# Differential attention with an expert layer on one core: where the attention rows are split into high and low parts, who combines the two maps, and which bank the query products use

## The reference

```python
A1 = jnp.einsum('bhqd,bhkd->bhqk', Q1, K1) * scaling
A2 = jnp.einsum('bhqd,bhkd->bhqk', Q2, K2) * scaling
attn = jax.nn.softmax(A1, axis=-1) - lam * jax.nn.softmax(A2, axis=-1)
O = jnp.einsum('bhqk,bhkd->bhqd', attn, V)
rms = jnp.sqrt(jnp.mean(O * O, axis=-1, keepdims=True) + EPS)
O = O / rms * rms_scale
...
return jnp.einsum('bne,de->bnd', O, Wo)
...
x = _layernorm(x + _L0_attn_ref(x, ...), axis=-1)
x = _layernorm(x + _L0_ffn_ref(x, ...), axis=-1)
```

## Time and profile before

| | |
|---|---|
| median of 3 runs | 1050.59 us (1050.27 to 1050.68) |
| profiled execution | 1053.84 us, span 1052.1 us |
| PE busy | 890.3 us (85%) |
| PEld busy | 720.4 us (68%) |
| POOL busy | 793.4 us (75%) |
| DVE busy | 766.6 us (73%) |
| ACT busy | 581.0 us (55%) |
| granted TensorE clock, mean | 0.925 |

### The profile page before, as it was taken

The page is one execution under the profiler, slowest core; times in us unless marked ns, Lnnn a source line. Parts: engine busy times, 40 slices in busy tenths (PEclk is TensorE's granted clock), DMA queues, the critical chain, the costliest instruction groups (busy, mean ns, idle before and its releaser), DMA issues.

```text
span 1052.1 us, 15341 instructions
## 1 busy us (share of the span) xinstructions
PE 890.3 (85%) x4365; PEld 720.4 (68%) x4366; DVE 766.6 (73%) x1185; ACT 581.0 (55%) x1090; POOL 793.4 (75%) x875
## 2 busy tenths in 40 slices
PE   6789999999999999999999999999999741258710
PEld 5567778887887788778877887878788531146510
DVE  6678778877887878788778878888788548536504
ACT  3546667666766576656766666766676331124300
POOL 2567888887988798888888888888799753375881
PEclk9899999999999999999999999999999955569955
DMA  2000000000000000000000000100000142011334
GB/s 70 1 11 11 1 1 19 3 1 0 20 0 0 10 10 0 0 10 10 0 0 10 10 0 0 50 0 0 1 1 1 53 130 65 19 51 26 33 35 122
DMA packets 36000, 20.67 MB, mean 20 GB/s; under 512 B 4560, under 2 KB 34416, under 8 KB 35968
## 3 DMA queue, kind: packets, MB, share of 16 engines
q1 hardware_dynamic: 30336, 15.95, 5.4%
q0 software_dynamic: 5632, 4.33, 3.0%
HBM read 13.85 MB, written 6.42 MB: 19 GB/s over the span
## 4 chain that ended last, share of the span: by engine, by line
PE 53%; issue 18%; DVE 16%; POOL 5%; ACT 3%; DMA 2%; another core or an unknown queue 2%; DVEq 0%; POOLq 0%; ACTq 0%; SPq 0%
PE t_ps L1074 7%; DVE negmax L760 6%; PE ring_a L1007 5%; PE ring_b L1007 5%; PE ring_a L1009 5%; PE ring_a L1008 5%; PE ring_b L1009 4%; PE ring_b L1008 4%; PE u_ps L1007 4%; PE u_ps L1008 4%; PE u_ps L1009 4%; POOL acc_dram L500 3%; ACT prob L572 2%; PE o_ps L1007 2%
## 5 line engine op out<-in xcount | busy, mean ns | idle before, releaser
L459 POOL TENSOR_TENSOR at_lo<-at,at_hi 128x1024 fp32r<-128x1024 f32 x127 | 308.6, 2430 | 0.8
L572 ACT ACTIVATE prob<-ring_a,negmax 128x1024 f32<-128x1024 f32 x128 | 142.8, 1116 | 252.7 <-DVE negmax L760 252.7
L431 POOL TENSOR_TENSOR s1sq<-psum 128x1 f32<-128x1 f32 x127 | 104.2, 820 | 125.2 <-ACT at L580 123.1
L828 DVE SCALAR_TENSOR_TENSOR attn<-prob,coef 128x1024 f32<-128x1024 f32 x128 | 180.1, 1407 | 5.1
L760 DVE TENSOR_REDUCE negmax<-ring_b 128x1 f32<-128x1024 f32 x128 | 155.6, 1216 | 4.7 <-PE ring_b L1009 1.7
L760 DVE TENSOR_REDUCE negmax<-ring_a 128x1 f32<-128x1024 f32 x128 | 155.7, 1216 | 1.3 <-PE ring_a L1009 0.2
L572 ACT ACTIVATE prob<-ring_b,negmax 128x1024 f32<-128x1024 f32 x128 | 142.8, 1116 | 20.3 <-DVE negmax L760 17.8
L434 POOL TENSOR_SCALAR at_hi<-at 128x1024 fp32r<-128x1024 f32 x127 | 141.4, 1114 | 0.0
L1074 PE MATMUL t_ps<-ident,attn 128*128 128x128 f32 x1024 | 134.4, 274 | 3.5 <-DVE attn L828 3.1
L1074 PEld LDWEIGHTS t_ps<-ident,attn 128*128 128x128 f32 x1024 | 118.9, 141 | 26.2 <-DVE attn L828 12.1
L580 ACT ACTIVATE at<-t_ps 128x1024 f32<-128x1024 f32 x128 | 130.2, 1017 | 2.7 <-PE t_ps L1074 2.7
(11 more groups left out here) (241 smaller groups left out, 1709.8 us busy)
## 6 DMA issues: line engine op xcount, KB each, us to landing
at<-in_L_ffn_w SPq DMA_DIRECT2D x16, 256.0 KB, 3.2
xres<-in_L_attn_X SPq DMA_DIRECT2D x2, 512.0 KB, 4.5
wq_s<-in_L_attn_Wq SPq DMA_DIRECT2D x8, 128.0 KB, 2.1
wk_s<-in_L_attn_Wk SPq DMA_DIRECT2D x8, 128.0 KB, 2.2
wv_s<-in_L_attn_Wv SPq DMA_DIRECT2D x8, 128.0 KB, 2.1
wo_s<-in_L_attn_Wo SPq DMA_DIRECT2D x8, 128.0 KB, 2.4
acc_dram<-zero SPq DMA_DIRECT2D x1, 1024.0 KB, 5.1
xg_dram<-xres SPq DMA_DIRECT2D x2, 512.0 KB, 3.4
```

The source lines that it names most:

```text
L431: pool.tensor_tensor(s1sq[:, r % TPH:r % TPH + 1], s1, s1, ALU.mult).then_inc(s1sq_ready, 1)
L459: pool.tensor_tensor(at_lo[:, g, :, c], src, at_hi[:, g, :, c].bitcast(F32), ALU.subtract).then_inc(at_split, 1)
L572: act.activation(prob[:, par, m, :], ring[m][:, :], ACT.Exp, bias=negmax[:, par, m:m + 1], accum_out=sums).then_inc(prob_ready, 1)
L828: dve.scalar_tensor_tensor(out=attn[:, par, :], in0=prob[:, par, 1, :], scalar=coef[:, par:par + 1], in1=prob[:, par, 0, :], op0=ALU.mult, ...
```

## The change

The transposes of a row come in two halves of four, both in the first bank of `t_ps`; ACT writes `at_hi` of a half straight from that bank (`at_high`) and DVE `at_lo` (`at_low`), so `at32`, the copy and POOL's two splits are gone. The second bank of `t_ps`, called `x_ps`, holds every extra product: a query chunk at the end of slots 0, 1, 3, 4 and 9, 11, 12, 15, m in 5, wt in 7, wp in 8; ACT and DVE read it at the beginning of the next slot. DVE's three operations of the combination go to POOL as five: a power (1/sum2) and two multiplications for the coefficient, a scaling of map 2 in place, and an addition. `attn` has four row buffers. The ages change: map 2's exponential one slot later (`LAG_E`), the coefficient 1, combination 2, transposes 2 and 3, product with x 7, output product 12, y 12, layer norm 0 two tail slots later. `es1` is made for four rows at once. Elsewhere `at32` is replaced by attn's buffers 2 and 3, whose loading waits for the last transposes.

```diff
 
-    LAG_T = 1
-    LAG_U = 6
-    LAG_O = 10
-    LAG_Y = 11
...
-
-    AT_QB, AT_WT, AT_WP, AT_M, AT_QA = (1, 2), 4, 6, 9, (11, 13)
-
-    AT_LN = (18, 19, 20, 21, 22)
...
+    LAG_E = 1
+    LAG_C = 1
+    LAG_S = 2
+    LAG_T1 = 2
+    LAG_T2 = 3
+    LAG_U = 7
+    LAG_O = 12
+    LAG_Y = 12
+    AB = 4
...
+    X_QB = {0: (0, 0), 1: (1, 0), 3: (0, 1), 4: (1, 1)}
+    X_M, X_WT, X_WP, AT_WW = 5, 7, 8, 11
+    X_QA = {9: (0, 0), 11: (1, 0), 12: (0, 1), 15: (1, 1)}
+
+    AT_LN = (20, 21, 22, 23, 24)
...
-        attn = sb("attn", [P, 2, N])
-        at32 = sb("at32", [P, 2, N])
+        attn = sb("attn", [P, AB, N])
...
         ring = [ps("ring_a", [P, N]), ps("ring_b", [P, N])]
         t_ps = ps("t_ps", [P, N])
+        x_ps = t_ps[:, NC:2 * NC]
...
+                r = i - LAG_S
...
+                    ts, sp = t - LAG_S, r % 2
                     s1 = psum1[:, r % TPH:r % TPH + 1]
+                    pool.wait_ge(coef_ready, ts + 1)
...
                     pool.tensor_tensor(s1sq[:, r % TPH:r % TPH + 1], s1, s1, ALU.mult).then_inc(s1sq_ready, 1)
-                    c = slice((r % GT) * P, (r % GT + 1) * P)
-                    src = at32[:, par, :].rearrange("p (k q) -> p k q", q=P)
-                    pool.tensor_scalar(at_hi[:, g, :, c], src, 1.0, 0.0, ALU.mult, ALU.add).then_inc(at_hi_done, 1)
-                r = i - LAG_O
+                    pool.tensor_scalar(prob[:, sp, 1, :], prob[:, sp, 1, :], coef[:, sp:sp + 1], None,
+                                       ALU.mult).then_inc(scaled_ready, 1)
+                    pool.wait_ge(scaled_ready, ts + 1)
+                    pool.tensor_tensor(attn[:, r % AB, :], prob[:, sp, 1, :], prob[:, sp, 0, :],
+                                       ALU.add).then_inc(attn_ready, 1)
...
+                    tc, par = t - LAG_C, r % 2
+                    need(pool, attn_ready, tc - 1)
+                    pool.wait_ge(prob_ready, 2 * tc + 2)
+                    pool.tensor_tensor(rs2[:, par:par + 1], psum2[:, par:par + 1], neg_one[:, :],
+                                       ALU.pow).then_inc(rs2_ready, 1)
+                    pool.wait_ge(rs2_ready, tc + 1)
+                    pool.tensor_tensor(coef_1[:, par:par + 1], rs2[:, par:par + 1], psum1[:, r % TPH:r % TPH + 1],
+                                       ALU.mult).then_inc(coef_1_ready, 1)
...
+                    pool.wait_ge(coef_1_ready, tc + 1)
+                    pool.tensor_tensor(coef[:, par:par + 1], coef_1[:, par:par + 1], neglam_h[:, :],
+                                       ALU.mult).then_inc(coef_ready, 1)
...
-                    pool.tensor_tensor(at_lo[:, g, :, c], src, at_hi[:, g, :, c].bitcast(F32),
-                                       ALU.subtract).then_inc(at_split, 1)
...
+            def q_round(h, which, m, c, src):
...
+                act.wait_ge(q_ready, q_count(h, which, m, c))
+                act.activation(q_hi[:, b, m, c * NC:(c + 1) * NC], src, ACT.Copy).then_inc(q_hi_done, 1)
...
+                def at_high(half, lag):
+                    r = i - lag
...
+                        act.wait_ge(t_ready, 2 * ta + half + 1)
...
+                        act.activation(at_hi[:, g, half * GT:(half + 1) * GT, c],
+                                       t_ps[:, 0:NC].rearrange("p (k q) -> p k q", q=P),
+                                       ACT.Copy).then_inc(at_hi_done, 1)
...
+                at_high(0, LAG_T1 + 1)
+                if not tail and i - 1 in X_QB:
+                    q_round(h, "b", *X_QB[i - 1], x_ps)
...
+                exponential(1, LAG_E)
...
-                    act.wait_ge(t_ready, tt + 1)
-                    need(act, at_split, tt - 1)
-                    act.activation(at32[:, r % 2, :], t_ps[:, :], ACT.Copy).then_inc(t_copied, 1)
...
+                at_high(1, LAG_T2)
+                exponential(0, 0)
...
+                def at_low(half, lag):
+                    r = i - lag
...
+                        dve.wait_ge(at_hi_done, 2 * ta + half + 1)
+                        dve.tensor_tensor(at_lo[:, g, k, c], t_ps[:, 0:NC].rearrange("p (k q) -> p k q", q=P),
+                                          at_hi[:, g, k, c].bitcast(F32), ALU.subtract).then_inc(at_split, 1)
...
+                at_low(0, LAG_T1 + 1)
+                if not tail and i - 1 in X_QB:
+                    q_part(h, "b", *X_QB[i - 1], x_ps)
...
+                at_low(1, LAG_T2)
+                if not tail:
+                    row_max(1)
...
-                    dve.reciprocal(rs2[:, par:par + 1], psum2[:, par:par + 1]).then_inc(rs2_ready, 1)
-                    dve.wait_ge(rs2_ready, t + 1)
-                    dve.tensor_scalar(coef[:, par:par + 1], rs2[:, par:par + 1], psum1[:, i:i + 1],
-                                      neglam_h[:, :], ALU.mult, ALU.mult).then_inc(coef_ready, 1)
-                    dve.wait_ge(coef_ready, t + 1)
-                    need(dve, t_ready, t - 1)
-                    dve.scalar_tensor_tensor(out=attn[:, par, :], in0=prob[:, par, 1, :],
-                                             scalar=coef[:, par:par + 1], in1=prob[:, par, 0, :],
-                                             op0=ALU.mult, op1=ALU.add).then_inc(attn_ready, 1)
...
+                def transposes(half, lag):
+                    r = i - lag
...
+                        if half == 0:
+                            pe.wait_ge(attn_ready, tt + 1)
+                        need(pe, at_split, 2 * tt + half)
+                        for k in range(GT):
+                            kk = half * GT + k
+                            last_t = pe.transpose(t_ps[:, k * P:(k + 1) * P], attn[:, r % AB, kk * P:(kk + 1) * P],
+                                                  ident[:, :])
+                        last_t.then_inc(t_ready, 1)
...
+                if not tail:
+                    scores(0, 0)
...
+                if not tail:
+                    scores(0, 1)
+                output()
+                transposes(1, LAG_T2)
+                if not tail:
+                    scores(1, 0)
+                    scores(1, 1)
+                r = i - LAG_U
...
+                    for k in range(j * PER, (j + 1) * PER):
...
+                transposes(0, LAG_T1)
+
+                if not tail and i in X_QB:
+                    m, c = X_QB[i]
+                    pe.wait_ge(q_split, q_count(h, "b", m, c) - 1)
+                    q_product("b", m, c, x_ps)
...
+                    m_product(h + 1, x_ps)
...
+                if i in X_QA and not last:
+                    m, c = X_QA[i]
...
+                    q_product("a", m, c, x_ps)
...
-                put_in = [i == AT_QB[0] and not tail, i == AT_QA[0] and not last, i == AT_WP and not tail,
-                          i == AT_M and not last]
-                if any(put_in):
-                    pe.wait_ge(prob_ready, 2 * t + 1)
```

More of the change, by code:

```diff
@@ L420, in slot @@
                 t = TPH * h + i
[L421 to L428 removed]
+                r = i - LAG_S
+                if exists(h, r, first) and r < TPH:
+                    ts, sp = t - LAG_S, r % 2
@@ new lines, in slot @@
+                at_low(0, LAG_T1 + 1)
+                if not tail and i - 1 in X_QB:
+                    q_part(h, "b", *X_QB[i - 1], x_ps)
+                if not last and i - 1 in X_QA:
+                    q_part(h + 1, "a", *X_QA[i - 1], x_ps)
+                if i == 0 and not first:
+                    q_part(h, "a", *X_QA[TPH - 1], x_ps)
+                if not last and i - 1 == X_M:
+                    m_parts(h + 1, x_ps[:, 0:2 * D])
+                if not tail and i - 1 == X_WT:
+                    dve.wait_ge(wt_ready, h + 1)
+                    need(dve, ww_installed, 2 * h)
+                    dve.tensor_copy(wwn_hi[:, 0:DV], x_ps[:, 0:DV]).then_inc(wt_hi_done, 1)
+                    for m in range(2):
+                        dve.tensor_scalar(wot_s[:, m, :], x_ps[:, DV + m * D:DV + (m + 1) * D],
+                                          rms_c[:, m:m + 1], None, ALU.mult).then_inc(wt_split, 1)
+                    dve.wait_ge(wt_hi_done, h + 1)
+                    dve.tensor_tensor(wwn_lo[:, 0:DV], x_ps[:, 0:DV], wwn_hi[:, 0:DV].bitcast(F32),
+                                      ALU.subtract).then_inc(wt_split, 1)
@@ L766, in slot @@
-                if r % GT == 0 and exists(h, r, first) and r < TPH:
-                    g = GPH * h + r // GT
-                    dve.wait_ge(u_hi_done, g + 1)
-                    dve.tensor_tensor(u_lo[:, :], u_ps[:, :], u_hi[:, :].bitcast(F32),
-                                      ALU.subtract).then_inc(u_split, 1)
-                if not tail:
-                    row_max(1)
                 if first and i == 0:
@@ L831, in slot @@
[L831 to L843 removed]
+                if i == 0 and not first:
+                    head_lambda()
@@ new lines, in output @@
+                def output():
+                    r = i - LAG_O
+                    if exists(h, r, first) and r < TPH:
```

(52 more changed lines are left out.)

328 lines of the change are left out of this document (136 added, 192 removed).

## The result

| | before | after |
|---|---|---|
| median | 1050.43 us, 4 runs (1042.34 to 1050.68) | 1192.89 us, 4 runs (1190.83 to 1195.81) |
| profiled execution, span | 1053.84, 1052.1 us | 1194.24, 1192.5 us |
| DVE, ACT, POOL busy | 766.6, 581.0, 793.4 us | 704.6, 592.1, 1022.7 us |

The change made the kernel slower: ratio of the mean times 1.138, 95% interval 1.132 to 1.144. The forecast was 1006 us.

The account below looks back on a forecast made before the run. TensorE was taken as the bound, at 95.6 us a head plus waits. Gains 15 + 25.8 + 4.2 + 0 = 45 us took 1053.8 to 1008.8 profiled, 1006 us median; forecast 999 to 1018, range 999 to 1036.

Parts of the forecast that it names:

- POOL's slot: POOL's work per slot after the change: 5.70 us, against TensorE's mean slot of 5.98, 0.28 us to spare.
- the one-input row: POOL's at_hi in the trace of before, 1.05 us, taken as the price of the new per-row scaling.
- the two-input row: POOL's at_lo in the trace of before, 2.40 us, taken as upper bound for the new scaling.
- rival 2: POOL becomes the bound: scaling at 2.40 us makes its slot 7.05 us, +102, 1153 us; chance 0.09.
- TensorE's price of a head: TensorE's work in one head, 16 slots of 5.54 us plus 7.0 us of extra products: 95.6 us.
- The gain of 25.8 us: Heads 1 to 6: the own bank removes TensorE's waits of 4.3 us a head.
- Head 0: First head, paced by POOL, then TensorE: 85.7 us against 102.3, 16.6 saved, taken as 15.
- Rival 3: Head 0 does not gain: ramp waits on hand-overs, 5.8 us a slot, 7 us lost, 1013 us; no separate chance given.
- Last head: The last head's 15 slot steps: 86.8 us instead of 91.0, 4.2 us gained.
- The handoff of the halves at nothing: Both transpose halves pass through one bank: 1.75 us under 1.9 us of cover, cost nothing, 0.15 us of room.
- Rival 1: The one bank of the two transpose halves becomes the wait: 1022 to 1038 us with 0.2 to 0.4 missing; chance 0.25.
- Tail: From the last scores to the second layer norm: 29.5 us against 30.7, counted as 0, between -2 and +3.

Follow-up runs that it names:

- the version with the second operation: The changed kernel with plus 0.0 added as second operation to POOL's scaling by the per-row coefficient: 1006.19 us, median of 5; ratio to before 0.963.
- two immediates: The changed kernel with POOL scaling map 2 by constant -0.25 and adding 0.0, per-row coefficient left out of the result: 1001.9 us.
- four forms of at_hi: The kernel before, POOL's at_hi written by slot number with an immediate or a column of ones, each with and without plus 0.0: 1122.1 us.
- the split version: The changed kernel, DVE combining columns 0 to 511, POOL the rest: 1004.13 us with a single-operation scaling, 1014.75 with two operations.

## Why the prediction was wrong

**The step that failed** is one term of POOL's slot: "Lower bound: the one-input row, 1.05 us; upper bound: the two-input row, 2.40. I take 1.05, since it reads one tensor and writes one like at_hi." It measured 2.86 us, above the upper bound too. I had chosen the row by the number of tensors, and asked only whether a per-row scalar differs from an immediate. At_hi's row was a pair of operations, times 1.0 and plus 0.0; the new instruction is a single one. The pair looked like two steps of which one is idle, and its plus 0.0 like a formality. The trace of before has no TENSOR_SCALAR with a single operation on POOL, so no row could price it. The range missed because it left out rival 2 altogether: even at its 2.40 us the time would have been 1153. Rival 2 had the mechanism right (POOL without gaps, the exponential of map 1 behind it) at a price of 2.40; its working with 2.86 gives 7.51 us a slot, measured 7.40. Its 127 slots at the full price overstate head 0, whose first slots lack var_o and fac (104.2 us): 940 us by the formula, 925.4 measured.

**The other steps**, read in the version with the second operation, whose profiled execution took 1006.19 us (span 1004.4). Row maxima of map 1:

```profile
L786 DVE TENSOR_REDUCE negmax<-ring_a x16: 1214/1225/1227, 22.5 to 100.2; 128x1 f32<-128x1024 f32 x16
L786 DVE TENSOR_REDUCE negmax<-ring_a x97: 1211/1225/1227, 106.6 to 680.4; 128x1 f32<-128x1024 f32 x97
L786 DVE TENSOR_REDUCE negmax<-ring_a x16: 1214/1225/1226, 680.4 to 767.3; 128x1 f32<-128x1024 f32 x16
```

- *TensorE's price of a head*, 95.6 us: (680.4 - 106.6) / 6 = 95.6. The gain of 25.8 us is there (25.7).
- *Head 0*: 84.1 us against 102.3, 18.2 saved where I had worked out 16.6 and taken 15. Rival 3 didn't come (and by its own figures it would have cost 7 x 5.8 - 34.7 = 5.9 us, not 7).
- *Last head*: 86.9 us; 86.8 was forecast.
- *POOL's slot*: 5.69 us, forecast 5.70. The scaling takes 1.13 rather than 1.05; the slot shown has no es, and smaller steps make up the rest. s1sq takes 0.19 us, undisturbed.
- *The handoff of the halves at nothing*: no wait of TensorE for at_lo stands in the table of waits from 107 to 680 us, which holds only waits of ACT, DVE and POOL. Rival 1 fell; with ACT busier by a scaling no such wait appears either.
- *Tail*: from the last of these starts to the second layer norm it is 805.72 - 767.3 = 38.4 us, against 844.00 - 812.8 = 31.2 before: 7.2 us lost where I counted 0 and at worst 3. Measured as in the earlier trace rows, from the last score matmul, it is 805.72 - 769.23 = 36.5 against 30.7; map 2's scores now come later in the slot, which is the other 1.4. My chain for it was too short (its terms add up to 29.4). POOL ended the last row 10.4 us after the scores, as I had said; but two halves through ACT and DVE, counted at 3.5, ended only 5.8 us later. So the last at_lo ends 16.1 us after the scores against 11.5 before, 4.7 of the 5.8 us. With the combination on DVE it was 16.3, so POOL's pace isn't the reason; the granted clock isn't either (0.91 in this stretch against 0.92 before, and with two immediates, at 1.00 throughout, from the last of the starts it took 36.8 us).
- *What no step spoke of*: behind that layer norm the profiled execution of before took 208.1 us and this one 198.7, for the same work. Most of it lies in the expert stage, whose low parts span 70.6 us in the one and 61.7 in the other:

```profile
L969 DVE TENSOR_TENSOR q_lo<-attn,q_hi x32: 691/693/768, 922.6 to 993.2; 128x512 fp32r<-128x512 f32 x32
```

```profile
L979 DVE TENSOR_TENSOR q_lo<-attn,q_hi x32: 691/693/768, 884.9 to 946.6; 128x512 fp32r<-128x512 f32 x32
```

In the kernel before with four forms of at_hi it was 61.2 us (1001.1 to 1062.3), and in all other profiled executions 60.5 to 65.9, so this is not the change but that one execution: before itself took anything from 1041 to 1053 us. The forecast took 45 us from a long one, 1053.84; against the runs of before beside it (1043.93) the version with the pair gains only 37.7. That it lands on 1006.19 is in part luck: between the two profiled spans the heads gain 48.0 us, the part ahead of them loses 2.5, and behind them the shorter expert stage, which the change didn't make, hides the tail's loss and leaves a gain of 2.2.

**The rule of the Trainium skill** (GPSIMD Engine Reference, 4.1 Engine selection) that spoke against the move holds by the outcome of the change as written. It adds that GpSimd is about at line rate with one input; the runs agree for a pair of operations and for a copy (1.05 and 1.04 us for 1024 columns) and disagree for a single operation (2.78). With the pair the move is right although POOL spends 3.5 us for DVE's 1.3, since POOL had them and TensorE is the bound either way. DVE's combination kept the heads at 95.6 us as well, so the move was not needed for the gain: that came from what the versions share, the own bank, the halves, the four row buffers and the new ages. No run takes these apart.

## What to carry to other kernels

A row prices an instruction only if it has the same form: the number of operations and the kind of each operand, not just the engine, the shape and the number of tensors. Where an engine is given work that leaves it a few per cent of room, make that one operand's price the first thing to measure, and put an upper bound on it that comes from outside the rows that look alike. And when an engine gets faster, ask what its work now lies beside: in the split version, with a pass shorter by 0.87 us, a head took 0.9 us longer.
